# Delta heads of a decoder layer: the block inverse is turned on VectorE, the second merge level runs as 32x32 products

## The reference

```python
retrieved = jnp.einsum('bhkv,bhk->bhv', Sstate, k_t)
error = v_t - g_t[..., None] * retrieved
update = k_t[..., :, None] * (beta_t[..., None] * error)[..., None, :]
Snew = g_t[..., None, None] * Sstate + update
o_t = jnp.einsum('bhkv,bhk->bhv', Snew, q_t)
```

## Time and profile before

| | |
|---|---|
| median of three runs | 3454.54 us |
| the profiled execution: span from first to last instruction | 3451.8 us |
| what the median has beside this span | 2.7 us |
| TensorE busy, whole span | 3232.5 us (94%), 19346 instructions |
| VectorE busy | 2178.8 us (63%), 4849 instructions |
| ScalarE busy | 1901.1 us (55%) |
| GpSimd busy | 1642.9 us (48%) |
| mean granted TensorE clock | 0.983 |
| first and last slot of the delta heads begin | 129.6 us and 1733.1 us |

### The profile page before, as it was taken

The page is one execution under the profiler, slowest core; times in us unless marked ns, Lnnn a source line. Parts: engine busy times, 40 slices in busy tenths (PEclk is TensorE's granted clock), DMA queues, the critical chain, the costliest instruction groups (busy, mean ns, idle before and its releaser), DMA issues. The chain is left out here.

```text
span 3451.8 us, 61234 instructions
## 1 busy us (share of the span) xinstructions
PE 3232.5 (94%) x19346; PEld 2587.3 (75%) x19346; DVE 2178.8 (63%) x4849; ACT 1901.1 (55%) x4657; POOL 1642.9 (48%) x3107
## 2 busy tenths in 40 slices
PE   6899999999999999999989888889989999998998
PEld 3688888888888888888878555568867777776443
DVE  5567767767677676676663388865447566575432
ACT  3677676766766767767632277744446454463111
POOL 3777777777787777777630000045543002011322
PEclk8899999999999999999999899999999999999999
DMA  4222222222222222222353333433342211211853
GB/s 118 57 72 68 56 67 66 71 68 62 60 67 69 69 63 70 69 52 69 86 175 97 126 113 141 166 101 103 117 140 94 79 68 69 80 71 46 277 97 59
DMA packets 432409, 310.49 MB, mean 90 GB/s; under 512 B 130496, under 2 KB 347456, under 8 KB 431072
## 3 DMA queue, kind: packets, MB, share of 16 engines
q1 hardware_dynamic: 423792, 289.57, 28.2%
q0 software_dynamic: 8432, 18.88, 2.7%
HBM read 177.97 MB, written 130.43 MB: 89 GB/s over the span
## 5 line engine op out<-in xcount | busy, mean ns | idle before, releaser
L636 PE MATMUL gd_PJ<-xn_lead,gd_w_rest 128*128 128x512 f32 x1024 | 421.5, 412 | 0.5 <-DVE gd_w_rest L799 0.5
L636 PE MATMUL gd_PJ<-xn_lead,gd_w_lead 128*128 128x512 f32 x1024 | 403.4, 394 | 0.0
L636 PE MATMUL gd_PJ<-xn_rest,gd_w_lead 128*128 128x512 f32 x1024 | 401.7, 392 | 0.0
L1091 POOL TENSOR_TENSOR gd_T<-gd_T,gd_prod 32x14 f32<-32x14 f32 (+6 forms) x896 | 317.0, 354 | 71.7 <-POOL gd_prod L1088 2.7
L1088 POOL TENSOR_TENSOR gd_prod<-gd_L,gd_T 32x14 f32<-32x14 f32 (+6 forms) x896 | 283.5, 316 | 71.0
L806 DVE SCALAR_TENSOR_TENSOR gd_conv<-gd_pre,gd_cur_a,gd_conv 128x512 f32<-128x512 f32 x384 | 301.0, 784 | 9.6 <-ACT gd_conv L967 2.7
L636 PEld LDWEIGHTS gd_PJ<-xn_lead,gd_w_lead 128*128 128x128 f32 x1024 | 193.6, 189 | 43.7
L636 PEld LDWEIGHTS gd_PJ<-xn_lead,gd_w_rest 128*128 128x128 f32 x1024 | 194.5, 190 | 38.5 <-DVE gd_w_rest L799 0.9
L636 PEld LDWEIGHTS gd_PJ<-xn_rest,gd_w_lead 128*128 128x128 f32 x1024 | 194.6, 190 | 35.2
L941 DVE SCALAR_TENSOR_TENSOR gd_og<-gd_B,ptab,gd_gate 128x512 f32<-128x512 f32 x64 | 48.0, 751 | 248.2 <-PE gd_B L650 248.2
L2628 ACT ACTIVATE sa_E<-sa_B,sa_nmax 128x512 f32<-128x512 f32 (+3 forms) x256 | 131.3, 525 | 131.6 <-DVE sa_nmax L2765 127.3
(11 more groups left out here) (477 smaller groups left out, 8792.5 us busy)
## 6 DMA issues: line engine op xcount, KB each, us to landing
expert_rows<-xt_blank SPq DMA_DIRECT2D x16, 2112.0 KB, 7.3
turned_queries_keys<-f_wq SPq DMA_DIRECT2D x16, 1280.0 KB, 6.0
x_wo<-decay_sums SPq DMA_DIRECT2D x64, 256.0 KB, 3.7
triangles<-gd_Lo SPq DMA_DIRECT2D x64, 256.0 KB, 3.4
gd_W<-turned_image SPq DMA_DIRECT2D x64, 256.0 KB
gd_T<-inverse_image SPq DMA_DIRECT2D x64, 256.0 KB
gated_outputs<-gd_og SPq DMA_DIRECT2D x64, 256.0 KB, 2.8
go_ogt<-gated_outputs SPq DMA_DIRECT2D x16, 1024.0 KB, 5.9
```

What stands on the lines that cost most here:

```text
L636: mm = pe.matmul(bank, w_parts[wp][:, j, k, :], rhs, start=(k == 0 and wp == 1), stop=(k == KT - 1 and wp + xp == 0))
L1091: nc.gpsimd.tensor_tensor(T16[:, rows, 0:j], T16[:, rows, 0:j], prod[:, rows, 0:j], ALU.subtract).then_inc(solving, 1)
```

## The change

The two turns of `W` on TensorE and the two copies into `T` are gone. In their place VectorE transposes blocks of 32x32 straight from SBUF (and one corner from PSUM) into a new tile `inv`: after the first merge level the first 64 rows and columns in one instruction and the third diagonal block of 32 in another (`turned_blocks`), after the second level the new corner block (`turned_corner`). An instruction of this kind transposes each 32x32 block in its place.

The second merge level no longer runs over the whole matrix. It has two pairs of 32-row blocks, at rows 0 and 64 (`PAIRS`, `UPPERS`). For each batch and pair there is one 32x32 product with 32 streamed columns, the two pairs writing to different PSUM banks; `masked(1)` is a negation and `merged(1)` a copy, each as two instructions over 32 rows. TensorE gets two instructions that raise a semaphore which nothing waits for (`blocks_open`), right after the waits that stand ahead of the new products. The third level's `merge` reads `inv` in place of `T`. `inv` is cleared once at the start.

```diff
+        inv = sb("inv", [P, B, TOP + TOP // 2])
+        SIDE = MERGE[1]
+        PAIRS = ((0, half[2]), (2 * SIDE, Bk[0][:, :, 0:SIDE]))
+        UPPERS = ((0, half[3]), (2 * SIDE, Bk[0][:, :, SIDE:2 * SIDE]))
...
# TensorE
+                    elif l == 1:
+                        pe.wait_ge(og_ready, n + 1)
+                        pe.sem_inc(blocks_open, 1)
+                        for b in range(B):
+                            for q, bank in PAIRS:
+                                lo, hi = slice(q, q + SIDE), slice(q + SIDE, q + 2 * SIDE)
+                                mm = pe.matmul(bank[lo, b, 0:SIDE], Lo_c[hi, b, lo], W_c[hi, b, hi], start=True, stop=True)
+                        mm.then_inc(y_sum, 1)
...
+                    pe.wait_ge(inv_ready, n * (NM - 1) + l)
+                    if l == 1:
+                        pe.sem_inc(blocks_open, 1)
+                        for b in range(B):
+                            for q, bank in UPPERS:
+                                at = slice(q, q + SIDE)
+                                mm = pe.matmul(bank[at, b, 0:SIDE], inv[at, b, q:q + SIDE], Y[at, l % 2, b, 0:SIDE], start=True, stop=True)
+                        mm.then_inc(wup, 1)
                     else:
+                        each(half[3][0:TOP], [inv[:, b, 0:TOP] for b in range(B)], [Y[:, l % 2, b, :] for b in range(B)], wup)
-                def turn_inverse(l):
-                    pe.wait_ge(w_ready, n * NM + l + 1)
-                    if l == 0:
-                        pe.wait_ge(og_ready, n + 1)
-                    turned(Bk[0], tiles(W_c), tup)
...
-                    turn_inverse(0)
                     spread_rows(1)
...
-                    turn_inverse(1)
                     spread_rows(2)
...
# VectorE
+                    if l == 1:
+                        for q, bank in PAIRS:
+                            at = slice(q, q + SIDE)
+                            ts = nc.vector.tensor_scalar(Y[at, l % 2, :, 0:SIDE], bank[at, :, 0:SIDE], -1.0, None, ALU.mult)
+                        ts.then_inc(y_ready, 1)
...
+                    if l == 1:
+                        for q, bank in UPPERS:
+                            tc = nc.vector.tensor_copy(W_c[q:q + SIDE, :, q + SIDE:q + 2 * SIDE], bank[q:q + SIDE, :, 0:SIDE])
+                        tc.then_inc(w_ready, 1)
...
-                def inverse_rows(l):
-                    s = MERGE[l]
-                    dve.wait_ge(tup, n * (NM - 1) + l + 1)
-                    nc.vector.tensor_copy(first(T_c, s), first(Bk[0], s)).then_inc(t_next, 1)
+                def turned_blocks():
+                    dve.wait_ge(w_ready, n * NM + 1)
+                    nc.vector.transpose(inv[0:TOP, :, 0:TOP], W_c[0:TOP, :, 0:TOP])
+                    at = slice(2 * SIDE, 3 * SIDE)
+                    nc.vector.transpose(inv[at, :, at], W_c[at, :, at]).then_inc(inv_ready, 1)
+                def turned_corner():
+                    nc.vector.transpose(inv[SIDE:2 * SIDE, :, 0:SIDE], half[3][0:SIDE, :, 0:SIDE]).then_inc(inv_ready, 1)
...
                     merged(0)
+                    turned_blocks()
...
-                    inverse_rows(0)
                     masked(1)
...
                     merged(1)
+                    turned_corner()
...
-                    inverse_rows(1)
                     masked(2)
...
+            nc.vector.memset(inv[:, :, 0:TOP], 0.0)
```

More of the change, by code:

```diff
@@ L36, in second @@
     return ap.rearrange("p b (g two m) -> p b g two m", two=2, m=m)[:, :, :, 1, :]
-def first(ap, m):
-    return ap.rearrange("p b (g two m) -> p b g two m", two=2, m=m)[:, :, :, 0, :]
 def bc(col, n):
@@ L510, in delta_heads @@
         solving, solved, cleared, masks_set = sem("solving"), sem("solved"), sem("cleared"), sem("masks_set")
-        y_sum, y_ready, wup, w_ready, tup, t_next = (sem(x) for x in ("ysum", "y", "wup", "w", "tup", "t"))
+        y_sum, y_ready, wup, w_ready, inv_ready, blocks_open = (sem(x) for x in ("ysum", "y", "wup", "w", "inv", "blocks"))
         ks_done, r_ready, oi_sum, oi_ready, u_sum, u_ready, o_sum, o_ready, s_sum, s_ready, sd_ready = (
@@ L668, in spread_rows @@
                         pe.wait_ge(w_ready, n * NM + l)
-                    if l < NM - 1:
+                    if l == 0:
                         each(half[2], tiles(Lo_c), [second(W_c, MERGE[l])[:, b] for b in range(B)], y_sum)
+                    elif l == 1:
[6 more added lines that the diff above has]
+                        mm.then_inc(y_sum, 1)
                     else:
@@ L677, in merge @@
                         pe.wait_ge(p_ready, n + 1)
-                    else:
-                        pe.wait_ge(t_next, n * (NM - 1) + l)
-                    if l < NM - 1:
-                        each(half[3], tiles(T_c), [Y[:, l % 2, b, :] for b in range(B)], wup)
-                    else:
-                        each(half[3][0:TOP], [T_c[:, b, 0:TOP] for b in range(B)], [Y[:, l % 2, b, :] for b in range(B)], wup)
-                def turn_inverse(l):
-                    pe.wait_ge(w_ready, n * NM + l + 1)
-                    if l == 0:
-                        pe.wait_ge(og_ready, n + 1)
-                    turned(Bk[0], tiles(W_c), tup)
+                        each(half[3], tiles(T_c), [Y[:, l % 2, b, :] for b in range(B)], wup)
+                        return
+                    pe.wait_ge(inv_ready, n * (NM - 1) + l)
[6 more added lines that the diff above has]
+                        mm.then_inc(wup, 1)
+                    else:
+                        each(half[3][0:TOP], [inv[:, b, 0:TOP] for b in range(B)], [Y[:, l % 2, b, :] for b in range(B)], wup)
                 if back and more and c == CH - 1:
```

## The result

The changed kernel takes 3439.89 us (median of four runs, 3436.21 to 3440.94). The kernel before, run beside it, takes 3456.34 us. The ratio is 0.9947 with a 95% interval of 0.9933 to 0.9961: faster, but by a third of the 50 us that were forecast, and above the forecast's range. The profiled execution spans 3439.1 us at a mean granted clock of 0.974.

What follows compares the result with a forecast made beforehand. TensorE, busy 497 of 500 us in the delta heads, was taken as the bound. 16 x (0.39 + 0.62 + 1.05 + 1.05) = 50 us; 3451.8 - 50 + 2.7 = 3405 us, range 3387 to 3436.

Steps and rivals of the forecast that it cites:

- TensorE's terms: Each slot: 2.54 us of transposes and second-level products removed, two small-product sets at 0.73 added, 0.25 of each for changing shape.
- VectorE's terms: Each slot: copies of T dropped, transposes at 0.42 and 0.29 and 32-row passes added; some 0.5 us more work.
- no idle of TensorE over 0.1 ahead of the third-level product in c = 2 and 3: Sign that the forecast is right: in these slots VectorE's W arrives in time, 3.41 against TensorE's own 3.46.
- some 0.5: Sign that the forecast is right: TensorE's idle in us ahead of the third-level product in c = 0 and 1.
- work taken from it comes back one for one, until another engine's answer is late: Basic step for the delta heads: TensorE, busy 497 of 500 us, ends the stage; alone it would give back 69 us.
- Other transfers stay: Claim that the remaining transfers are unaffected, with the c = 1 image landing at 973.1 and wanted at 973.76.
- These 0.64 hold the 0.39: The image's 0.64 us of slack in c = 1 slots covers the 0.39 by which c = 0 slots get shorter.
- Small products bound by issue: Rival: 32x32 products start 0.066 apart, a set costs 1.31, about 3459 us; midway 3422; chance 0.12.
- the row of 0.066: Earlier profile row of the only products from 32 rows to 32 columns, 0.066 us apart, used for the issue rival.
- Drains at the semaphore steps: Rival: TensorE runs out at its two new semaphore steps, 0.16 each, costing 10 us, 3415 us; chance 0.12.
- Slow transposes: Rival: VectorE's transposes ahead of tap and masks take up to four times the price, up to 3540 us; chance 0.06.
- The loss goes to GpSimd: Rival: GpSimd's solve plus fetch binds c = 1 slots, c = 0 gives nothing, 3411 us; shares the forecast's 0.70.

Runs made afterwards that it cites:

- row_first: Changed kernel, with GpSimd writing the next head's first key row ahead of starting its solve in c = 2 slots; 3427.47 us, ratio 0.9912.
- tri_first: Changed kernel, with SyncE storing the triangle ahead of the image fetch that waits for the inverse's store; 3418.02 us, ratio 0.9886.
- all_order: Changed kernel, with key row ahead of the solve, merged copies ahead of the diagonal, VectorE's two transposes behind the key's last tap; 3410.23 us, ratio 0.9867.
- short_solve: Changed kernel with four order changes (key row, merged copies, transposes, early triangle store) and GpSimd's solve two columns shorter; 3395.68 us, ratio 0.9820.
- order_tri: Changed kernel with four order changes: key row first, merged copies ahead of diagonal, transposes behind last key tap, early triangle store; 3402.71 us, ratio 0.9848.
- products_alone: Kernel before, with the second merge level as 32x32 products only, the inverse still turned by TensorE; 3458.43 us, ratio 1.0006.
- turns_alone: Changed kernel, with whole products again at the second level, VectorE still turning the blocks; 3431.89 us, ratio 0.9926.

## Why the prediction was wrong

**TensorE's terms.** 2.54 removed; 2 x 0.73 charged. A set costs 0.37 and some 0.1 to enter. Its products start 0.017 apart on average where I took 0.030 (sixteen starts within 0.25 us, where the prediction looked for 0.5), and the 0.25 for changing shape was too much. Error in the safe direction, and without effect, since TensorE no longer binds there.

**VectorE's terms.** 0.42 and 0.29 taken for the transposes, 0.44 and 0.30 measured; the corner 0.31 for 0.29. The passes over 32 rows took 0.28 each. Its chain was put at T + 3.41 in a c = 2 slot, just ahead of TensorE's 3.46. It came at 3.6, with TensorE there 0.53 earlier. So "no idle of TensorE over 0.1 ahead of the third-level product in c = 2 and 3" was wrong (0.5 to 0.6 there). The "some 0.5" for c = 0 does not follow from the sum's own times: they have TensorE free at T + 2.41 and the product at T + 3.93, which is 1.52; 1.69 came. Undisturbed slots are 0.44, 0.93, 0.95 and 0.83 shorter, 3.15 for a head against 3.11 forecast. That the two agree so closely is luck: c = 1 won 0.31 more than its term, c = 2 and 3 0.10 and 0.22 less.

**The step that failed** is "work taken from it comes back one for one, until another engine's answer is late". The sum took every slot at TensorE's full clock and looked for late answers in one place, the image of c = 1 slots. Neither holds. TensorE's idle in c = 0, 1.52 us by the sum's own times and priced as a wait alone, was 1.69 and was followed in nine of 14 heads by 3.41 us (once 6.83) at 1.2 GHz: 16.0 us lost, in a term that the sum put at nothing. In the kernel before TensorE's wait at this place, ahead of the second turn, was 0.5 at the most, once a head, and the clock was 1.00:

```profile
PE gd_B L650 <- DVE gd_W L830: 8.2, 16, 0.5
```

"Other transfers stay" was checked for the image fetch alone. Behind that fetch SyncE stores the triangle and fetches the blocks, GpSimd starts its solve and writes the key row, and the c = 2 keys hang on it, with two transposes of the change itself ahead of their last tap (7.2 us lost; row_first and tri_first each take it away). The prediction counted this delay of the keys in c = 0 and left it out in c = 2.

**"These 0.64 hold the 0.39"** held nearly in the changed kernel (c = 1 lost 0.8 us in all), because the other brakes kept the heads long. With these off it fails, as all_order's 25.88 and short_solve show: the solve itself is not a constant (11.76 us in c = 0 slots before, 13.03 in order_tri, with more steps beside taps).

**The last slot**, 7.7 us longer than before, was in no term: with all chunks shorter its image comes 2.14 late, and the slot as a whole runs at clock 0.65.

**The rivals.** Small products bound by issue: no, they start 0.017 us apart, and the row of 0.066 that it leaned on loads 128 columns of weights a product (32*128 in the earlier trace rows), not 32. (The 62 ns to issue that the Trainium skill states for matmuls that the sequencer's microcode handles, in "TensorE: Matmul & The Clock Gate", section "Wait — 56ns, not 53.3ns?", are not what these products show.) Drains at the semaphore steps: the key products take 1.08 up to the second set, 0.13 more than 0.95, which the change of shape (0.09 ahead of the first set) would account for nearly whole; no run parts the two. Slow transposes: no. "The loss goes to GpSimd" named an engine that did come late, but in the wrong place: the c = 1 slots lost 0.8 us in all, the keys of c = 2 and the last slot 15.7, and the other 16.0 went with the clock.

## What to carry to other kernels

When work is taken from the engine that is full, list what every other engine and queue has left in each slot, the transfers and their queue order included, and expect the first of these to become the bound at once; here two stood at about the same height, so that to take away the halved clock alone gave nothing, the late keys alone 12 us, and both 20. Look at idle that the change leaves on TensorE: here the halved clock followed it, and a shorter idle, by order of VectorE's work, was worth as much as dummy products. A part that gains nothing alone (products_alone) can gain 13 us once the waits around it are gone.

## What the runs showed of the hardware

- Float32 products of 32x32 with 32 columns, on two row groups in turn, start 0.017 us apart on average (16 starts within 0.25 us; the set holds TensorE for 0.37). VectorE's 32x32-block transposes in float32 take 437 ns for 64x256, 303 for 32x128 from SBUF and 306 from PSUM.
- GpSimd's small steps take 569 ns beside a VectorE tap and 259 otherwise; in order_tri, which packs VectorE more tightly, a solve took 12.38 us where it took 11.53 before.
- In c = 0 slots the granted clock fell to 0.50 behind an idle of 1.69 us in nine of 14 heads of the changed kernel, behind one of 1.22 in two of 15 (products_alone), and in none where the idle at that place was 1.0 to 1.1 (all_order) or 0.5 to 0.9 (turns_alone).
